# Flamingo block on Trainium2: keys and queries of one head pair in each piece of the projections, in place of long and short pieces in turn

## What is computed

```python
q_hk = (hidden_q @ Wq.T).reshape(b, s, H, K)
q_big = jnp.einsum('bshk,hkq->bshq', q_hk, w_kc_q)
...
kv_rope = kv_c * cos[None] + _rotate_half(kv_c) * sin[None]
q_r = jnp.einsum('bshq,hqr->bhsr', q_big, W_qr)
k_r = jnp.einsum('bld,hdr->bhlr', kv_rope, W_kr)
scores = jnp.einsum('bhsr,bhlr->bhsl', q_r, k_r)
attn = jax.nn.softmax(scores, axis=-1)
ctx_c = jnp.einsum('bhsl,bld->bhsd', attn, kv_rope)
...
x = x + jnp.tanh(g_xattn[0]) * _L0_xattn_ref(_layernorm(x, axis=-1), ctx_512, ...)
x = x + jnp.tanh(g_ffn[0]) * _L0_ffn_ref(_layernorm(x, axis=-1), ...)
```

## Time and profile before

| | us |
| --- | --- |
| median of 3 runs without a profile (1883.9 to 1887.91) | 1884.3 |
| the profiled execution | 1901.89 |
| its span, first to last instruction | 1900.1 |
| PE busy in it | 1833.7 (97%) |
| DVE busy | 1163.8 (61%) |
| ACT busy | 699.5 (37%) |
| POOL busy | 687.8 (36%) |

### The profile page before, as it was taken

How to read it: one execution, slowest core, us unless ns; L and a number is a source line. 1 busy time by engine, 2 the same in 40 slices (tenths; PEclk the granted TensorE clock), 3 DMA queues, 4 the chain that set the end, 5 groups by cost and what they waited for, 6 DMA issues and landing times.

```text
span 1900.1 us, 34773 instructions
## 1 busy us (share of the span) xinstructions
PE 1833.7 (97%) x12763; PEld 1124.7 (59%) x12946; DVE 1163.8 (61%) x2294; ACT 699.5 (37%) x1978; POOL 687.8 (36%) x714
## 2 busy tenths in 40 slices
PE   7899999999999998999999999999999899999998
PEld 7565666666666564444455555555544677667675
DVE  5677777777777776475422222222236788778887
ACT  4556666666666666220122222222211111111111
POOL 3245555555555656100233343343354521010101
PEclk9999999999999999999999999999999999999999
DMA  8546666766665767513399998999943422221202
GB/s 280 153 104 134 129 136 143 143 142 147 128 144 131 167 147 163 143 48 107 84 197 236 246 219 216 222 219 209 202 135 133 121 76 80 53 90 34 78 23 89
DMA packets 478930, 268.47 MB, mean 141 GB/s; under 512 B 410704, under 2 KB 416464, under 8 KB 478800
## 3 DMA queue, kind: packets, MB, share of 16 engines
q1 hardware_dynamic: 467280, 228.90, 51.9%
q0 software_dynamic: 11520, 37.76, 7.1%
HBM read 118.72 MB, written 48.23 MB: 88 GB/s over the span
## 4 chain that ended last, share of the span: by engine, by line
PE 81%; DVE 8%; ACT 3%; issue 3%; POOL 2%; DMA 2%; another core or an unknown queue 1%; SPq 0%; DVEq 0%; ACTq 0%; POOLq 0%
PE o L637 13%; PE o L911 8%; PE score L900 7%; PE p_bank L686 7%; PE o L832 5%; PE score L783 5%; PE score L766 4%; PE p_bank L900 4%; PE m_bank L900 4%; DVE arena L1130 3%; PE m_bank L783 3%; PE t_bank L832 3%; PE p_bank L783 3%; PE c_bank L832 3%; PE p_bank L766 2%
## 5 line engine op out<-in xcount | busy, mean ns | idle before, releaser
L637 PE MATMUL o<-arena 128*128 128x512 bf16 x1474 | 339.1, 379 | 4.5 <-DVE arena L1130 1.3
L1130 DVE TENSOR_TENSOR arena<-arena 128x512 bf16<-128x512 f32 (+3 forms) x357 | 306.5, 865 | 14.4 <-ACT arena L1023 4.4
L1575 POOL TENSOR_TENSOR arena<-arena 128x512 f32<-128x512 f32 x128 | 150.7, 1178 | 304.4 <-DVE arena L1151 302.3
L988 ACT ACTIVATE arena<-score,arena 128x128 f32<-128x128 f32 x512 | 181.9, 371 | 160.4 <-DVE arena L1222 160.4
L637 PEld LDWEIGHTS o<-arena 128*128 128x128 bf16 x1536 | 147.8, 98 | 156.1 <-DVE arena L1130 1.7
L686 PE MATMUL p_bank<-arena 128*128 128x256 bf16 x1536 | 180.4, 274 | 0.8 <-DVE arena L1130 0.7
L1660 POOL TENSOR_TENSOR arena<-arena 128x1088 bf16<-128x1088 f32 x32 | 72.0, 2249 | 275.1 <-ACT arena L1013 275.1
L911 PE MATMUL o<-arena 128*128 128x512 bf16 (+1 forms) x681 | 160.0, 379 | 3.9 <-DMA arena<-arena 1.9
L686 PEld LDWEIGHTS p_bank<-arena 128*128 128x128 bf16 x1536 | 146.0, 98 | 25.4 <-DVE arena L1130 1.3
L900 PE MATMUL score<-arena 128*128 128x352 bf16 x960 | 151.5, 315 | 2.9 <-issue 2.9
L783 PE MATMUL score<-arena 128*128 128x256 bf16 x1152 | 144.0, 273 | 3.5 <-DVE arena L1505 2.2
(11 more groups left out here) (208 smaller groups left out, 3171.4 us busy)
## 6 DMA issues: line engine op xcount, KB each, us to landing
xrow_d<-arena SPq DMA_DIRECT2D x80, 256.0 KB
arena<-w_expert SPq DMA_DIRECT2D x32, 544.0 KB, 5.7
arena<-w_shared SPq DMA_DIRECT2D x22, 384.0 KB, 3.7
arena<-x SPq DMA_DIRECT2D x16, 512.0 KB, 5.0
arena<-x SPq DMA_DIRECT2D x32, 256.0 KB, 3.1
x_d<-arena SPq DMA_DIRECT2D x32, 256.0 KB, 2.6
xn_d<-arena SPq DMA_DIRECT2D x32, 256.0 KB, 2.5
arena<-x_d SPq DMA_DIRECT2D x8, 1024.0 KB
```

Source lines behind the costliest of these rows:

```text
L637: mm = pe.matmul(o_bank[b % 2][:, :], lhsT=cT[u % 2][:, a, h, :], rhs=M_w[:, w, head_of(hg, h), :], start=(hg == 0 and n == 0), stop=(hg = ...
L988: mm = act.activation(prob[:, u % 4, h, :], score_bank[u % 2][:, h * S:(h + 1) * S], ACT.Exp, bias=neg_max[:, u % 4, h:h + 1], accum_out=d ...
L1130: return dve.tensor_tensor(dst, src, hi, ALU.subtract)
L1575: pool.tensor_tensor(prob[:, u % 4], prob[:, u % 4], rden[:, u % 4, :].unsqueeze(2).broadcast_to([P, 4, S]), ALU.mult).then_inc(normed, 1)
```

## The change

Each piece j now makes the keys and the queries of one head pair j: first 3 matmuls for the keys into columns 0 to 255 of the bank, then 12 for the queries into 256 to 511. The copy and the lower half write both with one instruction each, into a view `kq` that spans the keys' and the queries' regions, as two runs of 256 columns a fixed distance apart. The waits on the normalised x (xT1_in), on the rotation (ropeT_step) and on Kr_w (kr_lo) all stand before j = 0 now, resp. q = 0. ACT's wait for b_mm at q = 9 is gone. The waits of the scores on pr_lo are as before.

```diff
+        kq = halves(arena[:, k_at:2 * q_at - k_at]).rearrange("p (j r) -> p j r", j=2)
+
+        def kq_part(g, l, m):
+            at = (g % 2) * 4096 + l * 2048 + m * 256
+            return kq[:, :, at:at + 256]
+
...
-                    if q == 1:
+                    if q == 0:
                         pe.wait_ge(kr_lo, 1)
                     if j == 0:
                         wait(pe, xT1_in[g % 2], 32 * (g // 2 + 1), 32, it)
-                    if j == 1:
                         wait(pe, ropeT_step, 5 * (g + 1), 10, it)
-                    for half in range(2):
-                        mp = 2 * (j // 2) + half
-                        cols = slice(mp * P, (mp + 1) * P)
-                        o = piece_bank(q)[:, half * 256:(half + 1) * 256]
-                        if j % 2 == 0:
-                            for n in range(3 * KT):
-                                t, (a, w) = n // 3, PASSES[n % 3]
-                                mm = pe.matmul(o, lhsT=B_w[:, a, t, cols], rhs=xT1[g % 2][:, w, t, :],
-                                               start=(n == 0), stop=(n == 3 * KT - 1))
-                        else:
-                            for n, (a, w) in enumerate(PASSES):
-                                mm = pe.matmul(o, lhsT=Kr_w[:, a, cols], rhs=kvT[g % 2][:, w, :],
-                                               start=(n == 0), stop=(n == 2))
+                    cols = slice(j * P, (j + 1) * P)
+                    for n, (a, w) in enumerate(PASSES):
+                        pe.matmul(piece_bank(q)[:, 0:256], lhsT=Kr_w[:, a, cols], rhs=kvT[g % 2][:, w, :],
+                                  start=(n == 0), stop=(n == 2))
+                    for n in range(3 * KT):
+                        t, (a, w) = n // 3, PASSES[n % 3]
+                        mm = pe.matmul(piece_bank(q)[:, 256:512], lhsT=B_w[:, a, t, cols], rhs=xT1[g % 2][:, w, t, :],
+                                       start=(n == 0), stop=(n == 3 * KT - 1))
                     mm.then_inc(pr_mm, 1)
...
-                    jp = slice(2 * (j // 2), 2 * (j // 2) + 2)
-                    dst = (qT, kT)[j % 2][g % 2]
-                    if q == 9:
-                        act.wait_ge(b_mm, 4)
-                    act.copy(dst[:, HI, jp, :],
+                    act.copy(kq_part(g, HI, j),
                              piece_bank(q)[:, :].rearrange("p (m n) -> p m n", m=2)).then_inc(pr_hi, 1)
...
-                    lower(dst[:, LO, jp, :], piece_bank(q)[:, :].rearrange("p (m n) -> p m n", m=2),
-                          dst[:, HI, jp, :]).then_inc(pr_lo, 1)
+                    lower(kq_part(g, LO, j), piece_bank(q)[:, :].rearrange("p (m n) -> p m n", m=2),
+                          kq_part(g, HI, j)).then_inc(pr_lo, 1)
```

## The result

The changed kernel takes 1894.45 us (median of 6 runs, 1890.43 to 1896.84), beside 1883.68 us for the kernel before on the same chip (6 runs): a ratio of 1.0052, 95% interval 1.0042 to 1.0062, which is +7.9 to +11.7 us. It is slower, by as much as forecast. The mechanism is the one that the prediction gives; its main term was too large, as the traces show.

The account below looks back on a forecast made before the run. TensorE (PE) was taken as the bound, with 0.06 us to spare before one piece in eight steps. Waits 10.5, last groups +0.6 and start -0.3 sum to 10.8 us; 1884.3 + 10.8 = 1895 us, range 1886 to 1900.

Parts of the forecast that it names:

- main term: Steady attention, k = 8 to 88: the odd piece waits 0.95 us in each of 11 groups, 10.5 us.
- The step at which it happens: Steps with k mod 8 = 1: odd piece waits for DVE's lower half, 12 to 13 waits near 0.9 us, hardly elsewhere.
- That the wait comes back in each group: Eleven groups: the chain starts anew from PE's context at k mod 8 = 6, so each group pays again.
- ACT's copy at 431.00 ... may come some hundredths earlier: Step 62: copy stands close behind the long piece's end, so 0.95 us per wait was taken, a little under 0.98.
- The last groups: k = 96 and later: existing waits absorb lateness, 0.98 us more is made, less 0.38; +0.6 us, between 0 and 2.
- The start: Start-up: step -4's piece done 1.1 us earlier, step k = 0 costs most back; net -0.3 us, between -1.4 and +1.
- The two-run copies: Copies and lower halves writing two runs of 256 columns: priced at 0, upper end 3.3 us in all.
- A sign that wasn't met as it reads: Profile after the change: PE's busy time stays the same to 1 us.
- (b): Steady groups: bank free sooner than the profile says, waits of 0 to 0.4 us, 1884 to 1889 us; chance 0.13.
- (d): More waits: two-run copies cost 0.3 us a group, or k mod 8 = 4 waits too; 1898 to 1902 us; chance 0.07.
- (e): Each of the 11 waits brings PE's half clock, 17 us more, 1912 us; chance 0.03.
- (c): First 100 us: earlier even pieces let ACT copy sooner, at most 4.2 us faster, 1880 us; chance 0.05.

Follow-up runs that it names:

- e2: Changed kernel with only pieces 4 and 5 of each group long and short again; 1898.09 us, ratio 1.0004 to the kernel before.
- e6: Kernel before with only pieces 4 and 5 of each group made alike; 1909.75 us, ratio 1.0068 to the kernel before.
- e7: Changed kernel with pieces 4 and 5 of each group uneven, short one first, long one second; 1921.99 us, ratio 1.0130 to the kernel before.
- e4: Changed kernel with ScalarE's piece copy ahead of the exponentials in steps k mod 8 = 0 too; 1895.55 us, ratio 1.0001 to the kernel before.
- e5: Changed kernel run again without an edit; 1905.30 us, ratio 1.0048 to the kernel before.
- e1: Kernel before run again without an edit, as control and for a second profile; 1896.08 us, ratio 1.0000.
- e10: e8's kernel run again on another chip; 1881.56 us, ratio 0.9981 to the kernel before.
- e9: Kernel before, pieces still long and short, with e8's order of ScalarE's copies; 1885.22 us, ratio 0.9996 to the kernel before.
- e8: Changed kernel with ScalarE's copy ahead of the exponentials in k mod 8 = 0 and even start-up steps; 1893.70 us, ratio 0.9986 to the kernel before.

## Why the prediction was right, and where it was too large

**The step at which it happens: right.** Waits of the odd piece for the lower half in steps with k mod 8 = 1, 13 of them, and none at other steps. e2 and e6 show that the loss hangs on the pair there, e7 that it grows with the work taken from the even piece, and e4 that it is ScalarE's order that keeps the bank.

**That the wait comes back in each group: right.** The question on which I had made the sum rest is answered by +0.60, +1.33, ... +8.03. The chain is started anew from PE in each group (1.45 us idle of ScalarE before the context's copy at 432.49).

**The main term, 11 x 0.95 = 10.5 us: too large by a fifth.** It measured 11 x 0.75 = 8.3. The step that failed is "ACT's copy at 431.00 ... may come some hundredths earlier": it came 0.17 us earlier, since the end of the long piece did set that copy. The wait is 0.98 - 0.17 = 0.81 us (0.82 measured), and another 0.07 comes back in the group's other steps. I had looked only at the long piece of step 64, for which no term of the chain waits; the copy of the one of step 62 is in the chain too. In the rows it was to be read: 428.17 + 2.79 = 430.96 against a copy at 431.00, with no bracket, so that the timeline gives no idle time and no releaser. e6 shows it directly, with 3.50 us for a long piece and 3.33 for an alike one.

**The last groups, +0.6: +0.33 measured.** Of the 0.60 us that step 97 made, 0.27 was gone again by step 101, and all of the 0.46 of step 105 by step 109; the wait of the scores at 677.44 in the earlier trace rows is one that took it up.

**The start, -0.3: -0.2 measured,** but by luck as much as by the rows. The piece of step -4 was 2.6 us shorter, but the next two waits grew from 1.40 to 2.5 us and from 1.16 to 2.1 in the trace of after. The lower clock didn't go away either, it fell on the next piece:

```profile
77.90 2.77 PE L692 MATMUL p_bank<-arena 128*128 128x256 bf16 x12
```

In e5 the start-up had less of it, a granted clock of 0.97 in 50 to 100 us against 0.93, and its last piece came 7.0 us behind e1's in place of 8.4. What the start-up brings or costs thus differs between executions by a microsecond or more.

**The two-run copies, the keys' rotation, Kr_w, the wait for b_mm, at nothing: right.** Rows above for the first; the first piece of the changed kernel starts 0.24 us sooner than before. In e5 it is 0.62 later than in e1, which is the spread of the start-up: in both, as in the kernel before, no wait over 0.06 us stands before it. Only e4 has one, of 1.40 us for a lower half on VectorE, and its piece too starts at 41.10, as in the kernel before.

**The sum.** The terms measured come to 8.3 + 0.3 - 0.2 = 8.4 us, where I had 10.8. The medians say 10.8, with an interval of 7.9 to 11.7 that holds both numbers. So the agreement of 1894.45 with 1895 is in part luck, and closer than the working deserves.

**A sign that wasn't met as it reads.** PE's busy time was to stay the same to 1 us, and the page has 1833.7 us before and 1844.3 after. The page of before counts 12763 matmuls where that of after counts 12946, so the difference is one of missing records. With all 12946 in both, e1 has 1847.9 us and e5 1846.4. These are 1.5 us apart.

**The rivals.** (b), a bank free sooner than the profile says, is out: the medians lose as much as the traces show, or more. (d), more waits, is out by the rows. (e), the clock, is out: 1.00 from 100 to 600 us with 11 waits in it. The Trainium skill, "TensorE: Matmul & The Clock Gate", section "A second HAM failure mode: psum-queue depth-cycling", tells of a kernel whose short and frequent idles between matmul groups swing the clock. Here the idles are 0.6 to 0.8 us, once in some 43 us, and the trace shows no swing with them. (c), faster, did not come by itself, for the reason given: ScalarE's exponentials stand ahead of the copy. With that order changed it is e10, and its 3.3 us stand beside the 4.2 that I had put as the most.

**The 17.6 us between the profiled execution and the runs,** of which I couldn't tell where they lie, seem to lie neither in PE's pieces nor in the chain: the last piece of the kernel before stands at 717.13 and 716.72 in its two traces, though no trace of it is from a chip where it takes 1884 us. About 10 of the 17.6 are idle time of PE in the last part (16.5 us before, 6.7 in e9), as the last section shows.

## What to carry to other kernels

Making unequal pieces of work alike moves the deadline of what follows the longer one forward by the work taken out of it, and where one bank is handed from engine to engine the question is only whether that hand-over has this much to spare; here one step in eight had 0.06 us and the loss was 0.8 us there. Look then at what delays the hand-over: here a copy that could have run stood behind work that waited for another engine. Moving it ahead took the whole loss away (1.0048 to 1.0001), and with the same move at the start alike pieces were a gain of 0.2%. In the kernel before, where only one wait of 0.71 us behind the start hung on that copy, the same moves gave nothing that can be told from noise (0.9996). And take a row that starts within some hundredths of a microsecond after another engine's row has ended for a possible wait, though the timeline shows no idle time for it.

## What the hardware showed that I hadn't expected

In the last part of the kernel, which the change doesn't touch, VectorE stands for 3.3 to 3.6 us before one line of its program (L1505 in the kernel before), three times, some 82 us apart. What it could wait for had ended by the trace: PE's matmuls into the bank that it reads end at 1612.23 in the first of e1's. e1, the timelines of VectorE and of GpSimd:

```profile
1611.96 0.41 DVE L1501 TENSOR_TENSOR arena<-arena,score 128x256 f32<-128x256 f32 x1
1615.76 0.42 DVE L1505 TENSOR_TENSOR arena<-arena,p_bank 128x256 f32<-128x256 f32 x1 [3.39 <-remote]
...
1613.38 0.95 POOL L1732 DMA_INDIRECT arena<-xrow_d,arena  x1 [0.30 <-issue]
```

In the same trace it comes again at 1698.5 and 1781.3 us, and each time PE waits some 2.0 us. The stalls stand in all profiles of the runs e1 to e8 (three each) and in that of the kernel before that the prediction was made from, which has a fourth of 3.14 us at another line (L1497, at 1486.5). They stand in none of after, e9 and e10. Each of them lies at the end of a series of indirect DMAs that GpSimd issues (L1732): the three of each trace end 1.4 to 1.6 us after the last of eight such instructions, the fourth of before 1.0 after one. The same series are in the traces without stalls, though. In that of after one runs from 1612.85 to 1622.90, and VectorE comes to the same place of its program (L1501 there) without a stop:

```profile
1620.86 0.41 DVE L1501 TENSOR_TENSOR arena<-arena,p_bank 128x256 f32<-128x256 f32 x1
```

So the series may have a part in the stalls, and is not enough for one. PE's idle time behind 1480 us, in waits over 0.3 us, is 14.1 us in e1 and 6.7 in e9, 16.5 in the first profile of before and 5.8 in that of after. The medians of the kernel before go with it: 1896 us beside e1 to e8, 1884 to 1885 beside after, e9 and e10. Between chips and executions this is as large as what the whole change costs, and it is why only ratios from one chip are compared here. What makes the stalls, the runs don't show.

The other thing is in the start-up: the lower clock falls on different pieces from execution to execution. A long piece of 24 matmuls took 4.46 us in e9 and in e1 at steps -4, in e9 at -2 too, but 2.79 at -2 in e1; in e8 and e10, with pieces of 15 and the copies first, no piece met it, and 50 to 100 us had a granted clock of 1.00, but so it was in e6, with long pieces.
